# A transformer block's attention loop: another order of its jobs, loads first in the lead-in, the last stores of v on another queue

## What is computed

```python
h1 = _ln(x, n1_g, n1_b)
x = _attn(h1, h1, q1, k1, v1, o1_w, o1_b, heads) + x
h2 = _ln(x, n2_g, n2_b)
x = _attn(h2, context, q2, k2, v2, o2_w, o2_b, heads) + x
h3 = _ln(x, n3_g, n3_b)
proj = h3 @ ff_w1 + ff_b1
a, g = jnp.split(proj, 2, axis=-1)
ff = a * jax.nn.gelu(g, approximate=False) @ ff_w2 + ff_b2
return ff + x
```

## Time and profile before

| | us |
|---|---|
| median of three runs | 1295.64 (1292.84 to 1298.81) |
| the profiled execution | 1297.57 |
| its span, first to last instruction | 1295.8 |
| first stage | 0 to 150.42 |
| attention, lead-in | 150.42 to 198.83 |
| attention, 29 periods | 198.83 to 868.25 |
| attention, run-out | 868.25 to 935.90 |
| feed-forward | 935.90 to 1295.8 |

### The profile page before, as it was taken

One profiled execution on the slowest core, in us unless ns is written; L12 is line 12 of the kernel. 1 busy time (PEld: TensorE's weight loads), 2 busy tenths in 40 slices (PEclk: granted clock), 3 DMA queues, 4 the chain that ended last, 5 costly groups with the idle time before them and its releaser, 6 DMA issues. The chain is left out here.

```text
span 1295.8 us, 34279 instructions
## 1 busy us (share of the span) xinstructions
PE 1228.0 (95%) x12788; PEld 1135.1 (88%) x12788; DVE 828.9 (64%) x1606; ACT 671.4 (52%) x1622; POOL 601.5 (46%) x792
## 2 busy tenths in 40 slices
PE   6899769999999999999999999998799999999999
PEld 4899758888888888888888888886699999999999
DVE  5454447888888888888888888876565243332521
ACT  5565326666666666666666666664552322323131
POOL 5431125546555465555655546551564443423331
PEclk9999859999999999999999999999899999999999
DMA  4576645454555655556454554533021101010000
GB/s 128 192 236 215 217 124 157 133 175 130 150 158 160 187 153 176 158 165 186 132 168 135 148 166 134 164 110 98 26 60 37 36 11 41 0 51 0 25 1 26
DMA packets 105145, 154.49 MB, mean 119 GB/s; under 512 B 20780, under 2 KB 86564, under 8 KB 104996
## 3 DMA queue, kind: packets, MB, share of 16 engines
q1 hardware_dynamic: 104996, 152.49, 38.6%
HBM read 62.98 MB, written 28.93 MB: 71 GB/s over the span
## 5 line engine op out<-in xcount | busy, mean ns | idle before, releaser
L1419 ACT ACTIVATE probs<-expin 120x400 f32<-120x400 f32 (+2 forms) x635 | 297.5, 506 | 129.7 <-PE expin L812 126.0
L1096 DVE TENSOR_REDUCE neg_max<-score 100x2 f32<-100x722 f32 x320 | 288.0, 900 | 94.4 <-PE score L786 92.9
L812 PE MATMUL expin<-qs,ks 128*120 128x200 f32 (+2 forms) x1270 | 201.4, 272 | 3.8 <-DMA qs<-max_parts 1.8
L812 PEld LDWEIGHTS expin<-qs,ks 128*120 128x120 f32 (+2 forms) x1270 | 178.3, 181 | 16.3 <-ACT probs L1419 8.1
L786 PE MATMUL score<-ks,qs 128*100 128x362 f32 x640 | 170.5, 348 | 18.9 <-DVE neg_max L175 10.6
L2658 DVE SCALAR_TENSOR_TENSOR hidden<-ps_a,b_cols,gelu 128x320 f32<-128x320 f32 x100 | 55.1, 551 | 165.5 <-PE ps_a L2582 165.5
L2820 POOL TENSOR_TENSOR hid_lo<-hidden,hid_hi 128x320 fp32r<-128x320 f32 x100 | 88.1, 881 | 122.0 <-ACT hid_hi L2728 121.8
L1610 POOL MEMSET qs<- 128x2400 f32 (+1 forms) x58 | 112.6, 1941 | 69.0 <-PE expin L812 69.0
L2740 ACT ACTIVATE gelu<-ps_g,b_cols 128x320 f32<-128x320 f32 x100 | 52.7, 527 | 137.1 <-PE ps_g L2582 137.1
L786 PEld LDWEIGHTS score<-ks,qs 128*100 128x100 f32 x640 | 87.3, 168 | 40.5 <-issue 29.7
L834 PE MATMUL attn<-probs,vc 120*17 120x100 f32 (+1 forms) x3840 | 109.2, 253 | 0.0
(11 more groups left out here) (222 smaller groups left out, 2899.4 us busy)
## 6 DMA issues: line engine op xcount, KB each, us to landing
ks<-kc_parts SPq DMA_DIRECT2D x96, 362.0 KB, 3.7
qk_dram<-qk_parts SPq DMA_DIRECT2D x32, 500.0 KB, 5.4
qs<-q_parts SPq DMA_DIRECT2D x192, 75.0 KB
ks<-qk_dram SPq DMA_DIRECT2D x96, 125.0 KB
ctx_raw<-in_ctxT SPq DMA_DIRECT2D x64, 180.5 KB
ks<-kc_parts SPq DMA_DIRECT2D x96, 90.5 KB, 2.7
qs<-qk_dram SPq DMA_DIRECT2D x64, 125.0 KB
v_dram<-v_rows SPq DMA_DIRECT2D x32, 132.8 KB
```

What stands on the lines that cost most here:

```text
L812: mm = pe.matmul(dst, ks[a][u][:, k_slot(c) if a == 2 else c, j0:j0 + n], qs[a][u][:, :, q_slot(c) if a == 2 else c, :], start=True, stop= ...
L1096: ins = nc.vector.tensor_reduce(dst, src, AX_X, ALU.max, negate=True)
L1419: nc.scalar.activation(probs[e % NPT][0:n, :], expin[e % 2][0:n, 0:HG * N], ACT.Exp, scale=SCALE)\
```

## The change

In the first stage the last four stores of v are issued by ScalarE, each behind the copy after the one that it stores. In attention the five programs get another order in lead-in, period and run-out; no instruction of the computation is added or removed. Of batch c two exponent products (g = 1, 2) move from its own period's beginning to the end of the period before (where the batch is f), and the context projection VC (c, 1) moves from the end of the period to the beginning of the next (where the batch is s). `place_q2` and `turn_heads(2, ..)` move across the period's end too, but keep their place in their program's sequence. `load_x` loads one batch less ahead. The core of the diff:

```diff
 # first stage, SP and ScalarE
                 if k == 0:
                     head_rows(raw_o[1], given["o1"], landed["o1"])
-                else:
+                elif k < NK - 1:
                     store_values(k)
...
+            def store_last(i):
+                b = (NK - 1) * NB + i
+                act.wait_ge(v_made, b + 1)
+                act.dma_start(v1_dram[b], v_rows[i][:].rearrange("p h d -> p (h d)")).then_inc(v_stored[i], 16)
...
                 copy_values((NK - 1) * NB + i)
                 if i == 2:
                     heads_high()
+                if i:
+                    store_last(i - 1)
+            store_last(NB - 1)
 # attention, SP
             def lead_in():
+                load_x(1)
+                load_context(1)
+                set_key_rows()
                 load_qkv1(2)
-                set_key_rows()
                 place_max(1, 1)
-                load_context(1)
                 place_kc(0, 0)
                 place_q2(0)
-                load_x(1)
                 load_qkv1(3)
+                load_x(2)
                 place_max(1, 2)
-                load_x(2)
+                load_context(2)
                 place_kc(0, 2)
-                load_context(2)
                 place_kc(1, 0)
-                load_x(3)
+                place_q2(1)
...
             def period(x, s, c, f, e):
-                place_q2(s)
                 place_max(2, x)
                 if x is not None and 8 <= x < 8 + FF // P:
                     load_w1(x - 8)
+                place_kc(s, 2)
+                store_x2(v)
+                load_qkv1(e)
+                place_max(1, f)
                 load_context(f)
-                place_kc(s, 2)
-                load_x(e)
-                place_max(1, f)
-                load_qkv1(e)
-                store_x2(v)
                 place_kc(c, 0)
+                load_x(f)
+                place_q2(c)
 # attention, TensorE
             def lead_in():
+                project_out(1, 0)
                 self_scores(1, 0)
-                project_out(1, 0)
+                project_kc(0, 0)
+                self_scores(1, 1)
                 project_vc(0, 0)
-                self_scores(1, 1)
+                turn_normalised(0)
+                turn_max(1, 1)
+                project_q2(0)
+                project_kc(0, 1)
                 project_vc(0, 1)
-                turn_max(1, 1)
-                turn_normalised(0)
-                project_kc(0, 0)
-                project_kc(0, 1)
-                project_q2(0)
+                project_kc(0, 2)
+                turn_q2(0)
                 self_scores(2, 0)
-                turn_q2(0)
-                project_vc(0, 2)
                 scores_for_exp(1, 1, 0, 0)
                 scores_for_exp(1, 1, 1, 0)
-                project_kc(0, 2)
+                project_vc(0, 2)
                 scores_for_exp(1, 1, 2, 0)
...
+                cross_scores(0, 0)
                 project_kc(1, 0)
+                cross_scores(0, 1)
                 turn_max(1, 2)
-                cross_scores(0, 0)
-                cross_scores(0, 1)
                 cross_scores(0, 2)
...
+                scores_for_exp(1, 2, 1, 0)
+                project_kc(1, 2)
+                cross_scores(0, 9)
+                scores_for_exp(1, 2, 2, 0)
                 project_vc(1, 0)
-                project_vc(1, 1)
-                cross_scores(0, 9)
-                project_kc(1, 2)
...
             def run_out():
-                scores_for_exp(1, 31, 1, 0)
+                scores_for_exp(1, 31, 3, 0)
                 turn_max(2, 29)
-                scores_for_exp(1, 31, 2, 0)
+                project_vc(30, 1)
                 project_vc(30, 2)
-                scores_for_exp(1, 31, 3, 0)
                 scores_for_exp(1, 31, 4, 0)
...
+                cross_scores(30, 0)
                 project_out(2, 28)
-                cross_scores(30, 0)
+                cross_scores(30, 1)
...
             def period(x, s, c, f):
                 self_scores(f, 0)
-                scores_for_exp(1, c, 1, 0)
-                scores_for_exp(1, c, 2, 0)
                 turn_max(2, x)
+                project_vc(s, 1)
+                scores_for_exp(1, c, 3, 0)
                 project_vc(s, 2)
-                scores_for_exp(1, c, 3, 0)
+                self_scores(f, 1)
                 scores_for_exp(1, c, 4, 0)
-                self_scores(f, 1)
                 times_v(1, c, 0)
...
                 cross_scores(s, 0)
                 project_out(2, y)
-                turn_max(1, f)
                 scores_for_exp(2, x, 0, 0)
...
                 cross_scores(s, 4)
+                turn_max(1, f)
                 times_v(2, x, 0)
                 scores_for_exp(2, x, 2, 2)
                 scores_for_exp(2, x, 3, 0)
-                times_v(2, x, 1)
+                project_kc(c, 2)
                 cross_scores(s, 5)
                 scores_for_exp(2, x, 3, 1)
                 scores_for_exp(2, x, 3, 2)
                 turn_normalised(c)
-                project_kc(c, 2)
+                times_v(2, x, 1)
...
                 cross_scores(s, 8)
-                scores_for_exp(1, f, 0, 0)
                 times_v(2, x, 3)
                 times_v(2, x, 4)
                 cross_scores(s, 9)
+                scores_for_exp(1, f, 0, 0)
                 project_vc(c, 0)
-                project_vc(c, 1)
+                scores_for_exp(1, f, 1, 0)
+                scores_for_exp(1, f, 2, 0)
 # attention, VectorE, period and the end of run_out
-                max_low(1, f)
                 kc_low(c, 0)
...
                 maximum(2, s, 5)
+                max_low(1, f)
                 features_low("T2", c)
...
                 max_low(2, 31)
+                result(29)
+                tile_statistics(1)
                 normalise_tile(0)
...
+                result(30)
                 tile_low(1)
-                turn_heads(2, 31)
-                turn_back(2, 31)
+                result(31)
                 tile_low(2)
-                result(29)
-                result(30)
-                result(31)
 # attention, POOL, end of run_out and period
+                split_piece(0)
                 tile_deviation(0)
-                split_piece(0)
...
                 split_last(c)
+                first_residual(c)
                 scale_products(1, c)
                 clear_own(e)
                 heads_low(1, c)
                 inverse_deviation(c)
                 second_residual(c)
-                first_residual(e)
```

More of the change, by code:

```diff
@@ L46, in work_jobs @@
     y = None if x is None or x == 0 else x - 1
-    order = [("MT2", x, 0), ("VC", s, 2), ("O2", y, 0), ("MT1", f, 0), ("KC", c, 0), ("KC", c, 1), ("O1", c, 0),
-             ("T2", c, 0), ("KC", c, 2), ("Q2", c, 0), ("QT", c, 0), ("VC", c, 0), ("VC", c, 1)]
+    order = [("MT2", x, 0), ("VC", s, 1), ("VC", s, 2), ("O2", y, 0), ("KC", c, 0), ("KC", c, 1), ("O1", c, 0),
+             ("MT1", f, 0), ("KC", c, 2), ("T2", c, 0), ("Q2", c, 0), ("QT", c, 0), ("VC", c, 0)]
     return [job for job in order if job[1] is not None]
@@ L986, in run_out @@
                 scores_for_exp(2, 30, 4, 2)
-                project_out(2, 29)
+                times_v(2, 30, 2)
                 times_v(2, 30, 3)
@@ L1011, in run_out @@
                 times_v(2, 31, 4)
+                project_out(2, 30)
+                turn_tile(1)
                 turn_tile(2)
-                project_out(2, 30)
                 project_out(2, 31)
@@ L1257, in run_out @@
             def run_out():
+                turn_heads(2, 28)
+                turn_back(2, 28)
                 max_low(2, 29)
-                turn_back(2, 28)
+                maximum(2, 30, 0)
                 turn_heads(1, 31)
-                maximum(2, 30, 0)
+                maximum(2, 30, 1)
                 turn_back(1, 31)
-                maximum(2, 30, 1)
+                result(28)
+                maximum(2, 30, 2)
                 kc_low(31, 0)
-                result(28)
+                kc_low(31, 1)
                 second_input(31)
                 statistics(31)
-                maximum(2, 30, 2)
+                maximum(2, 30, 3)
                 normalise(31)
-                maximum(2, 30, 3)
+                maximum(2, 30, 4)
                 features_low("T2", 31)
-                maximum(2, 30, 4)
-                kc_low(31, 1)
                 maximum(2, 30, 5)
+                maximum(2, 30, 6)
                 q2_low(31)
-                maximum(2, 30, 6)
                 maximum(2, 30, 7)
-                kc_low(31, 2)
-                maximum(2, 30, 8)
-                maximum(2, 30, 9)
-                turn_heads(2, 29)
-                maximum(2, 31, 0)
-                max_low(2, 30)
-                maximum(2, 31, 1)
-                turn_back(2, 29)
+                maximum(2, 30, 8)
+                turn_heads(2, 29)
+                maximum(2, 30, 9)
+                max_low(2, 30)
```

(34 more changed lines are left out.)

169 lines of the change are left out of this document (82 added, 87 removed), and 12 rows, old and new, of the table DRAIN_EXP.

## The result

The changed kernel takes 1424.41 us (median of 4 runs, 1421.22 to 1427.06) against 1294.24 for the kernel before: ratio 1.0987, 95% interval 1.0962 to 1.1013. Forecast were 1286 us and a range that ended at 1299. It is slower by 130 us, beyond every rival but in the direction of (b).

The account below looks back on a forecast made before the run. TensorE was taken to bound the loop, SP's loads and placing largely the lead-in. Gains of 8.8 (lead-in) + 0 (loop) + 1 (drain) = 9.8 us gave 1287.8 for the profiled execution, forecast as 1286 us, range 1273 to 1299.

Parts of the forecast that it names:

- (b): Loop: SP falls behind at place_q2, its issue averaging over 5.0 us; up to 1312 us; slower 10%, no change 12%.
- The step that failed: Loop: loading the context later, since its split wants it only in the next period, was to cost nothing.
- The sum of place_q2: Loop, SP's queue: 16.95 + 4.09 + 1.70 = 22.74 us a period, 0.1 less than TensorE's own path.
- cross scores to start of place_q2: Loop, SP's queue: late maxima, context, keys and x come first, so place_q2 starts 16.95 us after the cross scores.
- its issue: Loop, SP's queue: issuing the six query DMAs of place_q2 takes 4.09 us, 5.33 at the longest.
- landing, to the next cross scores: Loop: placed queries land 1.70 us after their issue, and the next cross scores can start.
- TensorE's own path: Loop: the wait for the second self maximum is filled with work; a period takes 22.77 to 22.96 us, middle 22.85.
- (a): Loop: SP keeps ahead, query issue stays near 3.83 us, periods take 22.85; 7 us gained, 1279 us; chance 15%.
- The end of the first stage: ScalarE issues four last stores: block starts 1.9 us earlier, at 148.5; SP's wait for v ends at 153.5.
- The lead-in: Before the loop: SP's chain brings the first cross scores from 179.00 to 170.2 us, a gain of 8.8.
- (c): Lead-in: without TensorE's 4.37 us stall its clock stays high, 3.4 us more gained, 1282.6 us; chance 10%.
- The drain: After the loop: cross scores cover a 0.71 us wait and a store wait goes; net gain 1 us, bounds 4 either way.

Follow-up runs that it names:

- spread alone: The changed kernel with the second context load written as two transfers of 64 rows instead of one broadcast; 1330.43 us, ratio 1.0258.
- context early: The changed kernel with load_context(f) moved in SP's period from behind place_max(1, f) to ahead of load_qkv1(e); 1283.75 us, ratio 0.9906.
- the run with ScalarE's queue: The changed kernel with load_context(f) issued by ACT behind max_high(1, f), in the old one-broadcast form; 1303.83 us, ratio 1.0054.

## Why the prediction was wrong

**The step that failed** is one sentence: "The context's load moves later, but its split wants it in the next period only, as x is: both cost nothing." It asked who waits for the context, and not what waits behind it on the DMA engines. The sum of place_q2 priced only SP's issue of the load, 1.0 us. In its own terms, for the period from 524.91 to 552.72, and as means over the 28 steps of a loop from one batch's first cross scores to the next batch's (the loop's first period, which has no wait, is not in them):

| Term | Forecast | One period | Mean, changed kernel | Mean, spread alone |
|---|---|---|---|---|
| cross scores to start of place_q2 | 16.95 | 543.18 - 524.91 = 18.27 | 18.52 | 18.32 |
| its issue | 4.09 | 548.02 - 543.18 = 4.84 | 4.48 | 4.50 |
| landing, to the next cross scores | 1.70 | 552.72 - 548.02 = 4.70 | 4.68 | 1.74 |
| sum | 22.74 | 27.81 | 27.68 | 24.56 |

Landing is 3.0 of the 4.9 us that the mean is over the forecast, and with the load spread it is back at the forecast's size. Issue is 0.4, and that is not the two engines: it is as long with the load spread, and averaged 4.26 in the kernel before. The first term is 1.6 too small. In the kernel with the context early, whose TensorE hardly waits, place_q2 starts 532.46 - 516.06 = 16.40 behind the cross scores (mean 16.43), with 1.0 us less of issue ahead of it, so the chain's forecast was fair at full clock. In the changed kernel SP places the self maxima 12.75 us behind the cross scores on average, where 11.5 was forecast; with the load spread, whose loop has a clock of 0.99 instead of 0.93, it is 11.69. So the late maxima go with the half clock behind the wait, 0.50 in the window from 553 to 555 above; that the clock is what makes them late is argued, not tested.

**Rival (b)** had the right place and side by another mechanism: it moved one term, issue, up to 5.33, and issue averages 4.48. What grew is landing, which has no place in it, so that it pointed the right way is in part luck. The Trainium skill's rule quoted above, which gives this load two engines, was used neither there nor in the sum.

**TensorE's own path** was right. The wait for the second self maximum, 10.6 us before, is gone from the loop, also with the context early, where no wait for queries covers it. There a period takes 22.91 (forecast 22.85), so SP keeps up, as (a) had it, though its issue of the queries averages 4.13 us and not (a)'s 3.83; the time is 1283.75, between the forecast 1286 and (a)'s 1279. The lower bound of this path, 22.77, is a slip: its own terms go down to 23.04 - 0.35 - 0.02 = 22.67. Nothing rests on it.

**The end of the first stage.** ACT's stores were issued by 145.58, not 148.0; the block's first matmul came at 146.88, not 148.5. Yet SP goes on with its loads at 153.92, only 1.04 us earlier than before, where 1.5 was forecast, and it waits for something else by then. Its last wait there, before and after:

```profile
SPq L527 <- DMA v_dram<-v_rows: 4.5, 3, 3.8
...
SPq L529 <- DMA qk_dram<-qk_parts: 1.7, 1, 1.7
```

By the landing events of the traces, the last of v came at 152.88 instead of 154.87, and that of the queries and keys, which SP still stores, at 153.87 instead of 152.36. Timeline of the changed kernel, first stage's end and lead-in:

```profile
143.80 1.78 ACTq L2302 DMA_DIRECT2D v_dram<-v_rows  x2
...
147.23 1.91 SPq L145 DMA_DIRECT2D ctx_raw<-in_ctxT  x1
...
153.92 0.52 SPq L86 DMA_DIRECT2D qs<-zeros  x1
...
164.31 0.61 PE L813 MATMUL expin<-qs,ks 128*100 128x200 f32 x4
...
170.60 0.90 PE L787 MATMUL score<-ks,qs 128*100 128x362 f32 x2 [2.45 <-DMA qs<-q_parts]
```

From 146 to 150 us the DMA share is 0.94: what one transfer wins there another loses. The last issue moved 4.3 us (149.86 to 145.58) and the last landing a quarter of that, and even this is within the spread of the executions: in eight profiled ones with the new order SP goes on between 152.94 and 155.03, 154.4 on average, in four with the old between 153.60 and 154.96, 154.3 on average. So no gain of the stores' move shows here; the loads that now stand first in the lead-in use the same engines at that time, and no run tells the two apart. The Trainium skill's rule quoted in the forecast, that issuing from several engines saves the issue time alone, fits: on average the landing stayed.

**The lead-in** came as forecast here: exponents at 164.3 (163.7), first cross scores at 170.6 (170.2), loop at 188.17 (near 190). But the size is luckier than it looks. Eight profiled executions with this order of the lead-in start the loop between 188.17 and 192.15, 190.7 on average; four with the old order at 198.83, 195.07, 195.18 and 193.95, 195.8 on average. So the gain is nearer 5 than 10.7, and 198.83 was the latest of its kind. (c) comes and goes: with the same order the lead-in's clock is 0.82 in this trace, whose loop starts first of the eight, and 0.70 in that of the early context, whose loop starts 3.5 us later. What decides between them stays open.

**The drain.** Last period and drain together went from 90.68 to 98.50 us, with the queries late once more; with the context early they take 87.58, a gain of 3.1 where 1 (up to 4) was forecast.

## What to carry to other kernels

When a load is moved, price its packets on the DMA engines, not only its issue and its reader: count on how many engines its shape puts it, and ask what urgent transfer follows within the time that these need. Here the first context load, 128 packets over sixteen engines, landed 2.5 us after its issue began, and the second, a broadcast with an outer dimension of 2 and as many packets, 7.9 us after. Put such a load into a gap of the queue (here SP's wait for POOL, ahead of load_qkv1) or split it by rows. On an issue queue that feeds the bound engine every issue counts as well: three 4-byte loads of 1.0 us together cost 17.7 us over the early load alone (1301.47 against 1283.75).

## What the runs showed beside that

- The number of engines decides more than bytes: the same bytes in the same place cost 94 us more by two engines than by sixteen (1424.41 against 1330.43), one issue more included.
- How long SP takes to issue six query transfers varies from period to period, between 3.7 and 5.6 us, with a backlog on two engines and without: the means are 4.48 us with it, 4.50 with the load spread and 4.26 before. Single periods mislead here.
- A TensorE wait of 3 to 4 us is followed here by about 3 us at the lower clock (0.50 in the window from 553 to 555, 0.57 from 555 to 556, 1.00 behind), so it costs more than its length.
- The late pair works off one queue in its order: context, keys, x and queries one after the other until 551.9, while the other engines are through with the queries at 549. Between two queues it takes turns, as the run with ScalarE's queue shows.
- Three 4-byte loads took 0.99 us of SP's queue, 0.33 each; the same queue took 0.5 to 0.6 for an x load. ACT took 0.34 and 0.53 for the two context loads, where SP took 0.48 and 0.58 (in the periods shown).
